# Projection matmuls cut into row-half couples beside the scores, in rounds of 6, 6 and 12 steps

## What is computed

```
x = x + attention(layernorm(x));  out = x + ffn(layernorm(x))
attention: q, k, v = split(x @ w_qkv); 16 heads of 32; q and k of a head are two halves of 16
  a = softmax(q1 k1^T * s) - lam * softmax(q2 k2^T * s);  out = a @ v
  out / rms(out) * norm_w * 0.2, heads and time turned, then @ wo
ffn: h = x @ ternary(w_fc)^T + gate * (x @ v^T @ fast_b^T @ u^T);  out = relu(h)^2 @ ternary(w_proj)^T
```

## Time and profile before

| | before |
|---|---|
| median of 3 runs | 3755.79 us |
| profiled execution | 3755.76 us, span 3754.0 us |
| TensorE busy | 99% of the span |
| VectorE busy | 84% |
| ScalarE busy | 74% |
| GpSimd busy | 16% |
| chain that ended last | PE 88%, DVE 7%, issue 3% |
| pairs 2 to 55 | 184.59 to 2414.57 us |

### The profile page before, as it was taken

How to read it: one execution, slowest core, us unless ns; L and a number is a source line. 1 busy time by engine, 2 the same in 40 slices (tenths; PEclk the granted TensorE clock), 3 DMA queues, 4 the chain that set the end, 5 groups by cost and what they waited for, 6 DMA issues and landing times.

```text
span 3754.0 us, 57605 instructions
## 1 busy us (share of the span) xinstructions
PE 3705.5 (99%) x21704; PEld 2053.0 (55%) x21704; DVE 3152.0 (84%) x2927; ACT 2796.3 (74%) x3629; POOL 584.1 (16%) x269
## 2 busy tenths in 40 slices
PE   7999999999999999999999999999999999999999
PEld 6444444444444444444444444444468888888887
DVE  6899999999999999999999999988865555555554
ACT  4798888888888888888888989888863333333333
POOL 0101101023434343223223201210010000000000
PEclk9999999999999999999999999999999999999999
DMA  7544444445444444554554444534340101010010
GB/s 239 134 102 105 103 105 105 102 100 111 102 99 104 107 106 99 112 115 102 110 114 112 100 100 103 133 82 114 77 152 23 45 23 46 23 46 23 29 40 23
DMA packets 255350, 344.56 MB, mean 92 GB/s; under 512 B 118000, under 2 KB 142576, under 8 KB 254000
## 3 DMA queue, kind: packets, MB, share of 16 engines
q1 hardware_dynamic: 251504, 324.43, 36.6%
q0 software_dynamic: 3392, 15.73, 1.3%
q10 hardware_dynamic: 128, 0.03, 0.0%
HBM read 198.55 MB, written 131.07 MB: 88 GB/s over the span
## 4 chain that ended last, share of the span: by engine, by line
PE 88%; DVE 7%; issue 3%; DMA 1%; ACT 1%; SPq 0%; ACTq 0%; DVEq 0%
PE ps L875 22%; PE ps L850 16%; PE ps L940 13%; PE ps L995 12%; PE ps L786 9%; DVE acc L1632 5%; PE ps L926 4%; PE ps L789 4%; PE ps L896 3%; PE ps L945 2%; PE ps L758 1%; PE ps L1031 1%; PE ps L909 1%; PE ps L1016 1%; ACT pr L1261 0%
## 5 line engine op out<-in xcount | busy, mean ns | idle before, releaser
L1261 ACT ACTIVATE pr<-ps 128x1024 f32<-128x1024 f32 x2048 | 1989.8, 1029 | 257.0 <-PE ps L850 249.5
L1632 DVE TENSOR_TENSOR acc<-acc,pr 128x2048 f32<-128x2048 f32 x768 | 1780.9, 2319 | 40.3 <-ACT pr L1261 10.5
L875 PE MATMUL ps<-pr,vst 128*32 128x512 f32 x8192 | 1010.5, 599 | 0.3 <-DMA vst<-v_scratch 0.3
L850 PE MATMUL ps<-qst,kst 50*128 50x512 f32 x4096 | 781.9, 457 | 9.3 <-ACT pr L1261 6.9
L850 PEld LDWEIGHTS ps<-qst,kst 50*128 50x128 f32 x4096 | 337.1, 184 | 655.1 <-ACT pr L1261 460.1
L875 PEld LDWEIGHTS ps<-pr,vst 128*32 128x32 f32 x8192 | 213.4, 109 | 447.0 <-issue 436.6
L1430 ACT ACTIVATE rb<-ps,scf 128x512 f32<-128x512 f32 x228 | 157.0, 689 | 352.9 <-PE ps L945 352.9
L995 PE MATMUL ps<-tP,hh_ 128*128 128x512 f32 x1024 | 400.3, 391 | 0.6 <-DVE hl_ L1836 0.6
L995 PE MATMUL ps<-tP,hl_ 128*128 128x512 f32 x1024 | 399.5, 390 | 0.0
L786 PE MATMUL ps<-xt,wqh 128*128 128x512 f32 x1024 | 376.8, 419 | 3.0 <-DVE xt L1521 3.0
L940 PE MATMUL ps<-yh,tT 128*128 128x512 f32 x896 | 351.2, 392 | 0.0
(11 more groups left out here) (177 smaller groups left out, 3790.0 us busy)
## 6 DMA issues: line engine op xcount, KB each, us to landing
qst<-q_scratch SPq DMA_DIRECT2D x128, 256.0 KB, 4.6
kst<-k_scratch SPq DMA_DIRECT2D x128, 256.0 KB, 7.0
q_scratch<-stg SPq DMA_DIRECT2D x112, 256.0 KB
k_scratch<-stg SPq DMA_DIRECT2D x112, 256.0 KB
qst<-q_scratch SPq DMA_DIRECT2D x128, 128.0 KB, 4.9
kst<-k_scratch SPq DMA_DIRECT2D x128, 128.0 KB, 7.7
vst<-v_scratch SPq DMA_DIRECT2D x128, 128.0 KB, 4.6
xr<-in_L_attn_x_dram SPq DMA_DIRECT2D x64, 256.0 KB
```

The source lines that it names most:

```text
L850: ins = e.matmul(ps[:, 2 * c + hh, :], kst[rows, r, j, t * 128:(t + 1) * 128], qst[rows, r, j, c * 512:(c + 1) * 512], start=True, stop=True)
L875: ins = e.matmul(ps[32 * c4:32 * c4 + 32, 4 + j, :], vst[:, r, t, 32 * hh:32 * hh + 32], pr[:, sl, c, hh, :], start=(t == 0), stop=(t == 7 ...
L1261: e.activation(pr[:, sl, c, :, :], ps[:, 2 * c:2 * c + 2, :], ACT.Exp, scale=SCALE).then_inc(s_exp, 1)
L1632: e.tensor_tensor(acc[:, j, :], old, new, ALU.add).then_inc(s_add, 1)
```

## The change

The three projection tiles of a pair and the output projection of an earlier pair are no longer 48 matmuls over 128 rows. Each matmul over 128 rows becomes two over 64 rows, and two such halves of two different products are issued together as a couple, one in rows 0 to 63 and one in rows 64 to 127, each to its own bank. 24 couples hold tiles one and two (`c = 0`), 24 hold tile three and the output projection (`c = 1`). They stand in the same place of a round as the pieces before, but in rounds 0, 1 and 2 (6, 6 and 12 couples) and in rounds 4, 5 and 6 (6, 6 and 12); rounds 3 and 7 hold none. After the first twelve couples of 24 the two products change their row halves. This runs in pairs 2 to 55; pairs 0 and 1 have couples for `c = 0` only.

Around it: the softmax sums move from rounds 1 and 5 to 2 and 6 and into banks 4 and 5; `pe_part` moves from round 6 to 3, the transposes of the output from 3 to 7. ScalarE now copies both results of the v products out of PSUM (`act_raw`, two operations a pair) and no longer makes `oth`. GpSimd gets six operations of 128x512 a pair, five of which were VectorE's: `first_half`, `join_halves` (two), `scale_heads`, `output_low`, and `output_high` (`oth`), which was ScalarE's. The turned rows move on VectorE from round 6 to round 4. The stores on the SP queue move from rounds 2, 4, 6 to 4, 4, 7.

The core of the diff:

```
-PIECES = {0: (0, 0, 6), 1: (0, 6, 12), 2: (1, 0, 8), 3: (1, 8, 12), 4: (2, 0, 6), 5: (2, 6, 12)}
+WAVES = (0, 6, 12, 24)
...
+        def pe_couple(e, P, c, n0, n1):
...
+            for n in range(n0, n1):
+                h, u = divmod(n, 12)
+                if n == 12 and n0 < 12:
+                    e.wait_ge(s_half, 2 * P - 1 + c if P >= 2 else P + 1)
...
+                a = tile_half(e, T, 6, u, h, n == 0, n == 23)
+                if c:
+                    b = out_half(e, u, 1 - h, n == 0, n == 23)
+                else:
+                    b = tile_half(e, T + 1, 7, u, 1 - h, n == 0, n == 23)
...
-                    if d == 1 and P:
+                    if d == 2 and P:
                         pe_sum(e, P - 1, 1)
-                    if d == 5:
+                    if d == 6:
                         pe_sum(e, P, 0)
...
+                    if P < LOWP and d % 4 < 3:
+                        if d < 4:
+                            pe_couple(e, P, 0, WAVES[d], WAVES[d + 1])
+                        elif P >= 2:
+                            pe_couple(e, P, 1, WAVES[d - 4], WAVES[d - 3])
...
+                    if d == (3 if P else 7) and part_of(P):
                         pe_part(e, P)
-                    pe_posts(e, P, d)
+                    if d == 7 and P:
+                        pe_turn_out(e, P - 1, 4)
```

GpSimd's order in a pair, and two of its new operations:

```
+            for P in range(NPAIR):
...
+                if part_of(P):
+                    pool_part_apply(e, P)
+                if P >= 2:
+                    scale_heads(e, P - 2)
+                    output_high(e, P - 2)
+                if P:
+                    join_halves(e, P - 1)
+                if P >= 2:
+                    output_low(e, P - 2)
                 if SUM_P <= P < PROJ_P:
                     pool_magnitudes(e, 2 * (P - SUM_P))
...
+                first_half(e, P)
...
+        def join_halves(e, X):
+            e.wait_ge(s_rex, 2 * X + 2)
+            e.wait_ge(s_rw, 2 * X + 2)
+            e.tensor_tensor(ot[:], ot[:], rl[:, 1, :], ALU.mult).then_inc(s_pt, 1)
+            e.wait_ge(s_pt, 2 * X + 2)
+            e.tensor_tensor(ot[:], ot[:], rl[:, 0, :], ALU.add).then_inc(s_ot, 1)
```

`pe_pv` of step 8 (second softmax, bank 5) now waits for the turned rows of the same pair, which VectorE makes at the beginning of round 4:

```
+                elif part_of(P):
+                    e.wait_ge(s_xtl, turned(P) + 1)
```

More of the change, by code:

```diff
@@ L63, in rows_bank, with job_bank, out_bank, rank_bank @@
     return 6 + k % 2
-def sum_bank(P, j):
-    return 6 if j == 0 and P >= UPP else 7
+def job_bank(P, a):
+    return 6 + (5 * (P - UPP) + a) % 2
+def out_bank(X):
+    if X + 2 < LOWP or X + 2 >= NPAIR:
+        return 7
+    return job_bank(X + 2, 4) if X + 2 > LOWP else 6
+def rank_bank(n):
+    return {0: 7, 1: 5}.get(n, 6)
+def part_bank(P):
+    return 5 if P else 4
 def tile_of(m):
@@ L792, in pe_tile, with tile_half @@
                 t.then_inc(s_tile, 1)
-        def pe_flag(e, b, n):
-            bk = 6 if b else 5
[L797 to L803, removed]
-            else:
-                e.wait_ge(s_flv, 6 * b + 4)
-                e.matmul(ps[0:1, bk, 8:9], nfl[0:8, 4:5], ones[0:8, 0:1], start=True, stop=True).then_inc(s_flp, 1)
+        def tile_half(e, T, bk, u, h, first, last):
+            C, i = kind_of(T)
+            k, part = divmod(u, 3)
+            rows = slice(64 * h, 64 * h + 64)
+            w = (wqh, wql, wqh)[part]
+            xx = (xhi(C), xhi(C), xlo(C))[part]
+            if i < 8:
+                m0 = TILES[i] * 128
+                return e.matmul(ps[:, bk, :], w[rows, k, m0:m0 + 128], xx[rows, k, :], start=first, stop=last)
+            st = i - 8
+            return e.matmul(ps[:, bk, :], xx[rows, k, st * 128:(st + 1) * 128], w[rows, k, 2 * E:3 * E], start=first, stop=last)
@@ L808, in load_flag, with pe_flag @@
+        def pe_flag(e, b):
+            bk = 6 if b else 5
+            e.wait_ge(s_flv, 6 * b + 2)
+            if b:
+                tile_read(e, 24 + 3 * (b * NP - 1))
+            else:
+                e.wait_ge(s_xtl, 10)
+            for m in range(4):
+                t = e.matmul(ps[0:1, bk, 8 * m:8 * m + 8], nmx[:, 24 + m:25 + m], ind[:], start=True, stop=True)
+            t.then_inc(s_flp, 1)
         def load_flag(e, b):
@@ L1308, in act_posts, with act_out, act_out_square @@
-        def act_posts(e, P, d, half):
-            for a in range(3, 0, -1):
-                act_post(e, P - a, 8 * (a - 1) + d, half)
+        def act_out(e, X, bk):
+            e.wait_ge(s_tr, X + 1)
+            if X:
+                e.wait_ge(s_otl, X)
+            else:
+                e.wait_ge(s_lamv, 7)
+            e.activation(on[:], ps[:, bk, :], ACT.Copy).then_inc(s_raw, 1)
+        def act_out_square(e, X, bk):
+            if X:
+                e.wait_ge(s_ssq, X)
+            e.wait_ge(s_pt, 2 * X + 3 if X < NPAIR - 1 else 2 * NPAIR)
+            e.activation(sq[:], ps[:, bk, :], ACT.Square).then_inc(s_osq, 1)
@@ L1523, in dve_part_stats @@
         def dve_part_stats(e, P):
-            C, st = P // 4 + 3, P % 4
-            for n in range(P - 1, P) if P else range(-4, 0):
+            for n in range(P, P + 1) if P >= 0 else range(-4, 0):
                 if n < 0:
@@ L1675, in dve_posts, with dve_out_sum @@
[L1675 to L1682 removed]
+        def dve_out_sum(e, X):
+            e.wait_ge(s_osq, X + 1)
+            if X:
+                e.wait_ge(s_rmln, X)
+            e.tensor_reduce(ms[:, 0, :], sq[:].rearrange("p (g d) -> p g d", d=HD), AX.X, ALU.add).then_inc(s_ssq, 1)
@@ new lines, in vector_program @@
+                        if (d, half) == (0, 0) and P > LOWP:
+                            dve_out(e, P - 3)
+                        if (d, half) == (0, 1) and P >= 2:
+                            dve_out_sum(e, P - 2)
+                        if d == 2 and half == 1 and more:
+                            dve_low(e, 24 + 3 * P, 6)
+                        if d == 3 and half == 1 and more:
+                            dve_low(e, 25 + 3 * P, 7)
+                        if (d, half) == ((4, 0) if P else (7, 1)) and part_of(P):
+                            dve_turn_part(e, P)
@@ new lines, in vector_program @@
+                        if d == 4 and more:
+                            dve_bound(e, 24 + 3 * P + half)
+                        if (d, half) == (7, 0) and more:
+                            dve_low(e, 26 + 3 * P, 6)
+                            if P >= 2:
+                                dve_out(e, P - 2)
+                        if (P, d, half) == (0, 1, 1):
+                            dve_part_stats(e, -1)
+                        if (P, d, half) == (1, 1, 0):
+                            dve_part_stats(e, 0)
```

607 lines of the change are left out of this document (315 added, 292 removed).

## The result

The changed kernel takes 3848.65 us (median of 4 runs, 3847.25 to 3852.66) against 3755.59 (3754.76 to 3758.27) on the same chip: a ratio of 1.0248, 95% interval 1.0231 to 1.0266. It is slower by 93 us. The prediction was 3827, range 3775 to 3890.

The account below looks back on a forecast made before the run. It took a floor per round as the bound, PE only in the long rounds 2 and 6: 54 x (0.9 long round + 0.5 late turned rows) - 5 at the ends = +71 us on 3755.76, 3827 us; range 3775 to 3890.

Parts of the forecast that it names:

- The floor of a round: Each round lasts at least 4.82 us, 5.67 with softmax sums, through links between PE and ACT; work under it is free.
- The long round: Rounds 2 and 6, with sums and twelve couples: 6.59 us each over a floor of 5.67; the pair +0.9 us.
- The price of a change of kind: On PE, 0.20 us for each group of matmuls that starts after another kind.
- The sums and the long wave share a round: Reason given for less work but more time: softmax sums and twelve couples together in rounds 2 and 6.
- VectorE's late turned rows in round 5: PE's v products of step 8 wait for VectorE's turned rows: +0.5 us a pair, bounds 0 and 2.0.
- ScalarE 0: ScalarE's added copies, +0.65 us a pair, none on the path: cost 0, up to 0.2 a pair.
- VectorE's total: VectorE's work stays near 40 us a pair, as GpSimd's hold-ups cost about the 3 us it gave up.
- Outside the pairs: Outside the 54 pairs: -5 us, from pair 56 (-2) and after the last pair (-3).
- Pair 56 itself: Two banks in turn for the low-rank weights: -3 us at the most, taken as -2.
- the gain of 3 after the last pair: PE's 2.29 us wait for an add after the last pair now has a down product there: -3 us.
- the second: Rival: only the long round counts, GpSimd's operations fall into gaps: +44 us, 3800 us; chance 25%.
- the third: Rival: VectorE with GpSimd becomes the bound, 2.0 us in all 54 pairs or in 32: 3907 or 3863 us; chance 15%.

Follow-up runs that it names:

- e5: The kernel before, with four projection matmuls moved from round 3 to round 2, which then has twelve; no couples: 3800.14 us, ratio 1.0116.
- e11: e9 with SyncE's transfers that wait for GpSimd issued at step 6, behind the input load and shift rows: 3809.31 us, ratio 1.0135.
- e2: The changed kernel with rounds of 12, 6 and 6 couples instead of 6, 6 and 12: 3908.05 us, ratio 1.0403.
- e1: The changed kernel with rounds of 8, 8 and 8 couples instead of 6, 6 and 12: 3851.93 us, ratio 1.0253.
- e6: The changed kernel with rounds of 8, 8 and 8 couples, e4's cut of GpSimd's operations and e3's move: 3752.71 us, ratio 0.9986.
- e8: e7 with VectorE making the turned rows ahead of round 3's second running sum: 3806.85 us, ratio 1.014.
- e4: The changed kernel with GpSimd's six new operations cut from 512 to 32 columns in pairs 1 to 61: 3826.31 us, ratio 1.0186.
- e7: e1 with e3's move, and VectorE's low half and the flag's last part ahead of round 3's first running sum: 3816.69 us, ratio 1.0157.
- e3: The changed kernel with ScalarE's two small normalization operations moved behind round 0's third exponential, in every fourth pair: 3833.02 us, ratio 1.0202.
- e9: The changed kernel, 6, 6 and 12 couples, with the three moved steps of e8: 3836.89 us, ratio 1.0219.

## Why the prediction was right, and where it wasn't

**The floor of a round: right.** Round 0 (in most pairs) and round 1 are 4.82 with couples, as round 0 was with six single matmuls and as rounds with no projections were the earlier trace rows. e5 confirms it without any couples. PE's busy 99.8% didn't mean that taking work from it helps; it fell to 94.2% as the kernel got slower.

**The long round: right.** Forecast 6.59, measured 6.57. The pair's +0.9 us is 42.22 - 41.30 = 0.92 in e11, where nothing else is left: 54 x 0.92 = 50 of the 86 us. (Against a pair of before in which nothing is late it is 1.06 to 1.1; the change also took away waits that the kernel before had in rounds 1 and 5.) One couple at 0.229 is the 0.23 taken. The price of a change of kind was put together wrongly, though with the right sum: two score couples and the start of the next kind took 0.66 and 0.72 before (1508.99 - 1508.33 and 1511.30 - 1510.58) and take 0.56 each now, so 0.10 over the couples' 0.46, twice, where the formula has one 0.20. Why a change has become cheaper no run here tells.

**Its reason: wrong in one sentence.** "The sums and the long wave share a round" isn't the cause. e2 took them apart and got the same total for the two rounds (11.41 against 11.39). What costs is what goes beyond the idle time under a floor: eight couples are free, with sums (5.68 in e1) and without (4.84 in round 0 of e6), and the four beyond eight cost 4 x 0.229 = 0.92, the 0.90 by which rounds 2 and 6 exceed 5.67. The sum of the prediction has this right; only the sentence hasn't. With three eights a pair in which nothing is late takes 41.14 (e8), 1.06 less than with 6, 6 and 12, and no less than such a pair before, because of the two waits at the swap.

**VectorE's late turned rows in round 5: right place, too large.** Forecast 0.5, measured 0.23 (5.05 for 4.82). The rows were there when forecast, 26.9 us into pair 34 for "about 27"; it is PE that asks later than the 26.3 of the prediction, at 26.8, for the eight v products ahead of step 8's take 0.88 us, where the prediction had 0.45. In pair 34 of after the v products wait inside their group, 2.17 us for 1.92, for the turned rows L1665, made at 1586.59 behind a sum of 2.77 us and a low half that came at 1583.30. That it is GpSimd's doing is shown by e4, and that it is the next limit by e7, where it was 1.2 us a pair.

**What the prediction missed: 0.44 us a pair.** Round 0 in every fourth pair, 0.26 on the mean: "ScalarE 0" overlooked `act_part_ln`. The change moved it from round 2 to round 0, where it waits up to 0.9 us for VectorE's statistics, with a square and two exponentials behind it. I had walked the queue of VectorE but not asked who else waits for it (e3). Round 4, 0.18 on the mean: in every eighth pair the couples wait for the flag, made by VectorE behind the lengthened sums, and in pair 53 the same holds for the low half L1673 of a tile (e4). 0.92 + 0.23 + 0.26 + 0.18 = 1.59, the whole 86 us.

**VectorE's total: right.** 2171.95 / 54 = 40.2 us a pair for "near 40"; what it gave up came back in large part as longer sums (2540 for 2319 ns, 12 a pair: 2.7 us; forecast 3).

**Outside the pairs: wrong sign.** Forecast -5, measured +10.6. Of the +6.2 from pair 56 on, the turned rows take part: pairs 57 to 59 have a round of 5.5 in after and 4.82 from e8 on, and e11's stretch from pair 56 is 1341.9, 2.5 above before. Pair 56 itself is 1.2 shorter (forecast 2); the gain of 3 after the last pair wasn't found (1002.7 us from the last round's v products to the end, for 1002.2); and pair 57 begins with a round of 9.75 for 5.69, whose cause is open. Of the +4.4 to the beginning of pair 2, 2.3 is there before the first v product (110.02 for 107.68). That start also moves where nothing ahead of it was changed: e5, which is the kernel before up to there, has it at 111.21 in its execution. So a good part of the +4.4 can't be put down to the change. The other 2.1 falls into pairs 0 and 1, and its cause is open.

**The sum.** Long round 50 us (forecast 49), waits 36 (forecast 27), ends +11 (forecast -5): 97 for 71 on the profiled execution, 93 on the medians, and nearly all that was missing lies in the two smaller terms. That the waits come near is luck: of the 36 us only 12 are the wait that was forecast with 27, and 24 are the two that the prediction didn't have. Of the rivals, the second (only the long round, 3800) is e11's kernel, 3809.31 with its ends; the third (VectorE with GpSimd as the bound) isn't this kernel but is e1, e2 and e7: with 6, 6 and 12 the long round hides VectorE's lateness, which costs 1.3 us in round 4 as soon as the rounds are even.

## What to carry to other kernels

A busy share says how full an engine is, not what it would give back: split the period into its rounds, find one with little in it, and take its length as the floor; then work placed under a floor is free, work above it costs in full, and saved work under it is idle time. When work is moved from a nearly full engine to another, count what comes back to the first: here 2.7 us of sums for the operations that VectorE gave up. When one version takes the time of another, compare pairs in which nothing is late, and look for a new wait that has eaten the gain (here the swap). A kernel with several limits within 2% hides each behind the next: after each repair (e1, e7, e8) the time turned up one queue further, and only the table of rounds told where.

## What the runs showed of the hardware that I had not expected

- The same GpSimd operation (L462, 128x512, one input) takes 0.68 us or 2.81: 0.68 beside VectorE's reductions (e3, pair 40), 2.81 beside a running sum (e9). L464 takes 1.93 where it begins beside a reduction (after, pair 34) and 3.84 beside sums (e9). Moving one small operation in VectorE's order therefore made GpSimd 2.1 us late, and through a queue the kernel by four times 4.9 us (pairs 36 to 49 of e9: 45.10 + 44.2 for two of 42.2).
- GpSimd's 128x512 operations with two inputs take 1.83 to 3.27 us on the mean beside VectorE, for 1.27 in the two that ran free, and a sum beside them up to 3.2 us for 2.3: both sides pay.
- Couples of 64-row matmuls, one in each half, follow each other every 0.229 us, the pace of one 128-row matmul before (0.23), also over a run of twelve. Where the two products change their row halves and PE waits for its own last couple, it loses 0.33 us.
